# Maxima by bank, an even cut of the weighting products, and nineteen spare products in a two-layer perceiver kernel

## The reference

```
q = (norm(x) @ wq)   16 heads of 64
k = (ctx @ wk)       16 heads of 64
v = (ctx @ wv)       16 heads of 16
x = x + softmax(q k^T / 8) v, head by head
```

## Time and profile before

| | |
|---|---|
| median of 3 runs | 953.68 us (953.63 to 955.01) |
| the profiled execution | 953.95 us, its span 952.2 us |
| granted clock of TensorE, mean | 0.996 of full speed |
| TensorE busy | 923.3 us, 97% of the span |
| VectorE busy | 693.9 us, 73% |
| ScalarE busy | 574.6 us, 60% |
| GpSimd busy | 373.3 us, 39% |

### The profile page before, as it was taken

The page is one execution under the profiler, slowest core; times in us unless marked ns, Lnnn a source line. Parts: engine busy times, 40 slices in busy tenths (PEclk is TensorE's granted clock), DMA queues, the critical chain, the costliest instruction groups (busy, mean ns, idle before and its releaser), DMA issues.

```text
span 952.2 us, 30588 instructions
## 1 busy us (share of the span) xinstructions
PE 923.3 (97%) x13329; PEld 722.8 (76%) x13329; DVE 693.9 (73%) x872; ACT 574.6 (60%) x1408; POOL 373.3 (39%) x406
## 2 busy tenths in 40 slices
PE   7999999999999999999999999969989999999998
PEld 5677777777777777776667777758978787899998
DVE  4588888888888888788888888865036554368887
ACT  5666666666666666676666666624146663346764
POOL 2644444444444444444444444300123331513332
PEclk9999999999999999999999999989999999999999
DMA  6011101110110110000011000039758988409992
GB/s 238 24 26 26 26 25 25 26 25 25 25 25 25 25 25 25 25 25 25 25 25 26 19 9 3 3 128 397 256 194 273 283 274 275 170 2 319 324 333 92
DMA packets 78554, 98.10 MB, mean 103 GB/s; under 512 B 21584, under 2 KB 56928, under 8 KB 78432
## 3 DMA queue, kind: packets, MB, share of 16 engines
q1 hardware_dynamic: 77344, 94.67, 30.9%
q10 hardware_dynamic: 1088, 1.57, 0.5%
HBM read 95.68 MB, written 0.13 MB: 101 GB/s over the span
## 4 chain that ended last, share of the span: by engine, by line
PE 94%; DVE 3%; ACT 1%; DMA 1%; issue 0%; POOL 0%; ACTq 0%; DVEq 0%
PE ps L370 29%; PE ps L421 18%; PE ps L431 9%; PE ps L379 7%; PE ps L1594 6%; PE ps L1169 4%; PE ps L1071 3%; PE ps L1611 2%; PE ps L1615 2%; PE ps L1612 2%; PE ps L1158 2%; PE ps L287 1%; PE ps L1160 1%; PE ps L1159 1%; PE ps L1176 1%; PE ps L1417 1%
## 5 line engine op out<-in xcount | busy, mean ns | idle before, releaser
L681 DVE TENSOR_REDUCE x_peak<-ps 128x2 f32<-128x1024 f32 (+1 forms) x200 | 240.3, 1205 | 96.4 <-PE ps L421 87.7
L597 ACT ACTIVATE probs<-ps,x_peak 128x512 f32<-128x512 f32 (+1 forms) x400 | 266.2, 683 | 54.3 <-DVE x_peak L681 53.7
L700 DVE STREAM_TRANSPOSE probsT<-probs 128x1024 f32<-128x1024 f32 (+1 forms) x200 | 225.5, 1182 | 2.8 <-ACT probs L597 2.8
L421 PE MATMUL ps<-keys,qT 64*32 64x512 f32 (+1 forms) x3200 | 224.0, 585 | 1.4 <-ACT keys L584 0.6
L584 ACT COPY keys<-ps 128x512 f32<-128x512 f32 (+1 forms) x200 | 113.8, 583 | 144.1 <-PE ps L370 144.1
L431 PEld LDWEIGHTS ps<-probsT,vals 64*32 64x32 f32 x6016 | 116.8, 106 | 78.0 <-issue 73.3
L869 POOL TENSOR_SCALAR vals<-vals_t,x_side 128x512 f32<-128x512 f32 (+1 forms) x100 | 152.2, 1541 | 51.3 <-PEq L439 51.3
L370 PE MATMUL ps<-ctxT_hi,wk_hi 128*128 128x512 f32 (+1 forms) x400 | 157.4, 393 | 0.2 <-DVE wk_lo L734 0.2
L370 PE MATMUL ps<-ctxT_lo,wk_hi 128*128 128x512 f32 (+1 forms) x400 | 154.2, 385 | 0.0
L370 PE MATMUL ps<-ctxT_hi,wk_lo 128*128 128x512 f32 (+1 forms) x400 | 154.1, 385 | 0.0
L431 PE MATMUL ps<-probsT,vals 64*32 64x128 f32 x6016 | 131.5, 270 | 0.4 <-issue 0.4
(11 more groups left out here) (259 smaller groups left out, 1297.6 us busy)
## 6 DMA issues: line engine op xcount, KB each, us to landing
m_w<-in_m_w SPq DMA_DIRECT2D x32, 1024.0 KB, 7.6
ctx_raw<-in_ctxT SPq DMA_DIRECT2D x24, 512.0 KB, 3.7
ctx_two<-in_ctxT SPq DMA_DIRECT2D x24, 512.0 KB, 4.0
ctx_one<-in_ctx SPq DMA_DIRECT2D x24, 512.0 KB, 5.1
x_shrinkT<-x_shrink SPq DMA_DIRECT2D x384, 1.0 KB, 1.7
f_h1T<-in_f_h1T SPq DMA_DIRECT2D x1, 4096.0 KB, 18.5
f_h2T<-in_f_h2T SPq DMA_DIRECT2D x1, 4096.0 KB, 28.2
m_shared_w<-in_m_sw SPq DMA_DIRECT2D x2, 1024.0 KB, 7.4
```

Source lines behind the costliest of these rows:

```text
L421: i = pe.matmul(m.ps[32 * j:32 * (j + 1), score_bank(t) + odd, 0:nt * P], m.qT[rows, 4 * group + j, qs], m.keys[rows, 4 * group + j, 0:nt ...
L597: return act.activation(m.probs[t][:, odd, 0:nt * P], m.ps[:, score_bank(t) + odd, 0:nt * P], ACT.Exp, bias=m.peak[slot][:, 1, 2 * (t // H ...
L681: dv.tensor_reduce(m.peak[slot][:, 1, cs, t % HALF], m.ps[:, bank:bank + 2, 0:nt * P], AX.X, ALU.min).then_inc(s["dve" if t == STEPS - 1 e ...
L700: i = dv.transpose(m.probsT[:, cs, 0:4 * nt, t % HALF * 32:t % HALF * 32 + 32], m.probs[t][:, :, 0:nt * P].rearrange("p c (b k) -> p c b k ...
```

## The change

Three edits.

1. `maxima` takes two instructions in place of one, the even bank first and then the odd one, and each signals `max_ready` (in the last step the second signals through `dve`, as the one instruction did before). `exponentials` waits for `max_ready` once more, between its two exponentials.
2. `BLOCK_CUTS` puts two blocks of weighting behind each of the eight steps (one behind each in the first full chunk).
3. In the last chunk TensorE runs 19 spare products behind the wait for `out_kept`.

```diff
-BLOCK_CUTS = (0, 3, 5, 8, 10, 12, 14, 16, 16)
+BLOCK_CUTS = (0, 2, 4, 6, 8, 10, 12, 14, 16)
...
         else:
             output_turned()
+            spare_products(pe, m, OUT_BANK, 19)
...
     def exponentials(slot, t, nt):
         act.wait_ge(s["max_ready"], n("max_ready"))
         exponential(slot, t, 0, nt).then_inc(s["even_ready"], 1)
+        act.wait_ge(s["max_ready"], n("max_ready"))
         exponential(slot, t, 1, nt).then_inc(s["probs_ready"], 1)
...
     def maxima(slot, t, nt):
         dv.wait_ge(s["scores_full"], n("scores_full"))
-        cs = slice(2 * (t // HALF), 2 * (t // HALF) + 2)
-        bank = score_bank(t)
-        dv.tensor_reduce(m.peak[slot][:, 1, cs, t % HALF], m.ps[:, bank:bank + 2, 0:nt * P],
-                         AX.X, ALU.min).then_inc(s["dve" if t == STEPS - 1 else "max_ready"], 1)
+        for odd in range(2):
+            last = t == STEPS - 1 and odd == 1
+            dv.tensor_reduce(m.peak[slot][:, 1, 2 * (t // HALF) + odd, t % HALF:t % HALF + 1],
+                             m.ps[:, score_bank(t) + odd, 0:nt * P], AX.X,
+                             ALU.min).then_inc(s["dve" if last else "max_ready"], 1)
```

## The result

| | before | changed |
|---|---|---|
| median of 4 runs | 953.65 us (952.67 to 955.01) | 947.38 us (946.55 to 948.19) |
| the profiled execution | 953.95 us, span 952.2 | 947.57 us, span 945.8 |

The ratio is 0.9926 (95% interval 0.9909 to 0.9943): 7.1 us or 0.7% faster (the two medians differ by 6.3). The forecast was 4.3 us.

What follows compares the result with a forecast made beforehand. TensorE, busy 97% of the span, was taken to bound the kernel. The terms 0.8 + 0.4 + 0.2 + 2.0 + 0.9 sum to 4.3 us, giving a median of 949.4 us, range 947.0 to 953.6.

Steps and rivals of the forecast that it cites:

- the wait at steps 6 and 7: Quiet chunks: TensorE's scores wait for ScalarE, 0.07 us a chunk; removing it in about 12 chunks gains 0.8 us.
- VectorE's pair at 1.29: Maxima of a step: two 512-element reductions overlap and take 1.29 us together, against 1.23 for one of 1024.
- ScalarE's start: Exponentials of a step: the even one starts 0.54 us earlier, and ScalarE keeps its pace of 1.34 us.
- the margin of 0.27: Step 7 of a quiet chunk: scores may start at 245.47, TensorE's loads come at 245.74, so the wait is gone.
- The rival in which VectorE sets the pace: Maxima of a step: two reductions without overlap cost VectorE 1.38 us, over TensorE's 1.30; 952.9 us, chance 0.08.
- The irregular loss: 6.2 us in 11 of 22 periods, from late packets in the steps; even cut gains 2.0, at most 4.4.
- The move of two blocks at no cost of its own: Even cut: two blocks (0.44 us) move from behind steps 0 and 2 to behind step 7, priced at zero.
- The last chunk: Last weighting: earlier transposes 0.67 us, start behind VectorE 0.1, clock from spare products 0.2; gain 0.9, down to 0.4.
- The waits only: Score steps: late packets cost the same wherever the blocks stand, leaving a gain of 2.3 us; 951.4 us, chance 0.27.
- The slower one: Score steps: packets come later still, each of 23 chunks stalls 0.56 us, loss 12.9 us; 958.1 us, chance 0.10.

Runs made afterwards that it cites:

- run 4: Kernel before with 32 small products ahead of the first chunk, shifting TensorE's records by 128: ratio 1.0020 to the kernel before.
- run 2: Changed kernel with the old block cut and without the spare products, so the maxima by bank alone: ratio 0.9976 to the kernel before.
- run 3: Changed kernel without the 19 spare products: ratio 0.9942 to the kernel before.
- run 7: Changed kernel without spare products, blocks cut early as 4, 4, 2, 2, 2, 2, 0, 0: ratio 1.0043 to the kernel before.
- Run 9: Changed kernel with 11 and 6 more spare products, so TensorE has no pause in the last chunk: ratio 0.9912 to the kernel before.
- run 5: Changed kernel again, unaltered, on another chip: ratio 0.9922 to the kernel before.
- run 8: Changed kernel with 7 more spare products between the halves of the last weighting: ratio 0.9918 to the kernel before.
- run 10: Changed kernel with the later cut of blocks, 1, 2, 2, 2, 2, 2, 2, 3: ratio 0.9922 to the kernel before.

## Why the prediction was right or wrong

- **The bound, and the wait at steps 6 and 7.** Right. TensorE bounds the kernel, the 0.07 us for a quiet chunk was 0.06, and it went in all 22 periods and not in 12 (1.3 us for 0.8).
- **VectorE's pair at 1.29, ScalarE's start, the margin of 0.27.** Right: VectorE keeps TensorE's pace and the quiet chunk shows no wait. The rival in which VectorE sets the pace did not come.
- **The irregular loss: the step that failed.** The text priced the even cut's effect on it as "each stall can shrink by up to that", 0.4 us for 11 chunks, and took the middle, 2.0; the profiles went from 6.2 to 0.4 us, 5.9 less. The mechanism, packets of instructions that come late in the dense steps, was right, and the term was mis-sized, for three reasons.
  - *The split maxima's share was put at nothing.* With them alone the loss is 3.5 us, after 6.2 and, in run 4, 5.2 with the old maxima. I had not foreseen this, and no run explains it; one profile with an us or more of spread does not carry far. The even cut on top brings it to 0.4 to 2.2 in four profiles, so 1.3 to 3.1 us less, around the 2.0 of the forecast; by ratio it is 3.2.
  - *A miscount.* With the even cut 288 products' records are out after 8.01 us, as the text has it, but the scores of step 6 add 16, not 32. So 304 are out after 8.87 us and 320 after one more block of 0.22, at 9.09. The same instruction is wanted 0.67 us later, not 0.4; that makes the most 7.4 us instead of 4.4, the middle 3.7 and the forecast 6.0 us.
  - *One instant was compared*, the records used up to step 6, as if a stall depended on that alone. Runs 2, 3 and 7 order the loss by how fast the first steps use instructions: 0.4 to 2.2 us for 96, 96, 96 records a step, 3.5 for 128, 96, 128, and 12.7 for 160, 160, 96. Between the last two it grows by 9 us, 0.4 in each chunk, for 64 more records in the first three steps; I had allowed that much only for the chunks that already stalled and then halved it.
- **The move of two blocks at no cost of its own.** Right: the wide phase began earlier. But the text added up the parts as if each were worth the same without the others, and it is not so: the even cut alone costs 2.1 us, behind the split maxima it gains 3.2. The sum should have asked what each part is worth without the other.
- **The last chunk.** Wrong in sign, +0.4 for -0.9. The transposes came 0.56 us earlier, as worked out (0.67). But I put the clock at full speed after the spare products, and it fell behind them: the second half, which nothing hides, took 1.1 us more. The Trainium skill (TensorE: Matmul & The Clock Gate, HAM oscillation — how this bites in real kernels) advises to avoid pauses so that the array stays at the higher level. Run 9, with no pause left, agrees: its clock stayed at 1.00 through this stage. Runs 5 and 8, with pauses left, fell to the lower level; but run 10 has pauses of 1.74 and 1.71 us and kept the higher one, so what decides it with pauses of this length is not shown.
- **Behind the last chunk** 0.6 us were lost that no term had. The stretch from 692 to 790 us (699 to 796 before) took 97.3 us after 96.7, with a granted clock of 0.72 from 700 to 710; the profile of before shows no low clock in its stretch. All the other profiles but that of run 8 had a few us of lower clock there too, so I count it to that one profile of before, not to the change.
- **The rivals.** None came. "The waits only" had 951.4. The slower one asked for a loss of 12.9 us, and run 7 lost 12.7; but it has another cut, with denser first steps, and that the two numbers are alike is chance. Packets over 3.4 us apart are the rule in all profiles, and the even cut still lost less. The median of 947.38 lies at the fast edge of the stated range.

## What to carry to other kernels

A hand-ordered stretch of small tiled products can outrun its own instructions: look for "issue" gaps in the weight loads with no semaphore behind them, number the engine's records to see whether the gaps come at one place in a block, and spread short instructions evenly before removing anything. Price two edits together and apart, since one may only pay once the other has opened the room. Spare products that are to keep a clock up can merely move the low stretch onto work that matters more; look at more than one profile before counting on them.

## What was not expected of the hardware

- The instruction queue costs time on the engine that runs straight-line code: up to 1.11 us in a single gap, 12.7 us in a kernel of 958. All twenty gaps of over 0.6 us stood at the same place in a block of 256 records. The queue itself is busy 0.7% of the span.
- The same products in another order, 4, 4, 2, 2, 2, 2 blocks in place of two everywhere, take 1.2% more of the whole kernel.
- The lower clock level came after pauses of 2.0 and 1.7 us with 7.2 us of work between them, and in run 10, with pauses of 1.74 and 1.71 us, it did not come.
